# Attention in a fused network: value blocks moved by two steps, denominators before values, bf16 casts of q and k on ScalarE

## What is computed

```
x_ln = layer_norm(x_flat, g1, beta1)
qkv = x_ln @ w_qkv.T
q, k, v = jnp.split(qkv, 3, axis=-1)
...
scores = jnp.einsum('bhqd,bhkd->bhqk', q, k) * HEAD_DIM ** (-0.5)
attn = jax.nn.softmax(scores, axis=-1)
out = jnp.einsum('bhqk,bhkd->bhqd', attn, v)
```

## Time and profile before

| | us |
|---|---|
| median of three runs | 3499.21 (3495.88 to 3499.93) |
| the profiled execution | 3492.03 |
| its span, first to last instruction | 3490.3 |
| attention: ACT's first exponential to its last | about 102 to 1792 |
| one middle period of attention | 52.37 |

### The profile page before, as it was taken

How to read it: one execution, slowest core, us unless ns; L and a number is a source line. 1 busy time by engine, 2 the same in 40 slices (tenths; PEclk the granted TensorE clock), 3 DMA queues, 4 the chain that set the end, 5 groups by cost and what they waited for, 6 DMA issues and landing times. The chain is left out here.

```text
span 3490.3 us, 54609 instructions
## 1 busy us (share of the span) xinstructions
PE 3056.1 (88%) x17526; PEld 1156.3 (33%) x17526; DVE 2526.1 (72%) x3282; ACT 2045.6 (59%) x2445; POOL 2163.6 (62%) x876
## 2 busy tenths in 40 slices
PE   5999999999999999999957999556887788877877
PEld 2333333333333333333312333422232222222222
DVE  4888888888788888888812221236898889898888
ACT  3577777777677777777732332235556545655554
POOL 0588888888778888888870000016666766676665
PEclk7899999999999999999979999778999999999999
DMA  3577777777767777777763210134343434434343
GB/s 108 121 170 173 185 170 178 184 172 172 172 168 177 176 179 172 176 185 173 170 149 111 94 42 12 63 116 152 124 154 126 146 129 143 146 127 163 109 158 121
DMA packets 111603, 503.25 MB, mean 144 GB/s; under 512 B 17184, under 2 KB 18276, under 8 KB 78516
## 3 DMA queue, kind: packets, MB, share of 16 engines
q0 software_dynamic: 32704, 218.17, 29.9%
q1 hardware_dynamic: 78676, 282.17, 23.5%
HBM read 192.42 MB, written 39.39 MB: 66 GB/s over the span
## 5 line engine op out<-in xcount | busy, mean ns | idle before, releaser
L565 DVE TENSOR_REDUCE at_pmax<-at_ring 128x1 f32<-128x512 f32 x2048 | 1289.2, 685 | 280.2 <-PE at_ring L356 279.0
L527 ACT ACTIVATE at_probs<-at_sc 128x1024 f32<-128x1024 f32 x1024 | 992.5, 1021 | 371.1 <-PE at_sc L423 369.6
L615 POOL TENSOR_TENSOR at_prob_sums<-at_prob_sums,at_probs 128x2048 f32<-128x2048 f32 x192 | 907.1, 4725 | 72.2 <-ACT at_probs L527 71.9
L416 PE MATMUL at_sc<-at_QT,at_KT 32*128 32x512 f32 x4096 | 774.4, 632 | 8.3 <-issue 7.1
L1695 POOL TENSOR_TENSOR ss_drive<-ss_du,ss_bsb 128x1024 f32<-128x1024 f32 x261 | 610.7, 2353 | 263.4 <-DVE ss_state L1652 256.6
L1595 ACT ACTIVATE ss_decay<-ss_delta,ss_a 128x512 f32<-128x512 f32 x520 | 354.5, 687 | 446.9 <-DVE ss_state L1648 298.9
L435 PE MATMUL at_O<-at_probs,at_V 128*32 128x512 f32 x4096 | 536.2, 607 | 1.1 <-ACT at_probs L527 1.1
L1484 PE MATMUL ss_Y<-ss_seen,ss_ident 128*128 128x512 f32 x1032 | 520.1, 628 | 0.0
L356 PE MATMUL at_ring<-at_KH,at_QH 32*128 32x512 bf16 x2048 | 430.1, 387 | 6.9 <-DVE at_pmax L565 4.0
L1660 DVE TENSOR_TENSOR ss_seen<-ss_state,ss_C 128x1024 f32<-128x1024 f32 x259 | 316.3, 1221 | 78.7 <-PE ss_C L1472 70.8
L1652 DVE TENSOR_TENSOR_SCAN ss_state<-ss_decay,ss_state,ss_drive 128x512 f32<-128x512 f32 x259 | 332.3, 1283 | 33.6
(11 more groups left out here) (195 smaller groups left out, 2847.7 us busy)
## 6 DMA issues: line engine op xcount, KB each, us to landing
ss_bsb<-scratch_rows SPq DMA_DIRECT2D x265, 512.0 KB, 6.9
at_odd_sums<-at_probs POOLq DMA_DIRECT2D x128, 1024.0 KB, 7.6
at_odd_sums<-at_probs SPq DMA_DIRECT2D x64, 1024.0 KB, 4.8
at_prob_sums<-at_odd_sums POOLq DMA_DIRECT2D x64, 1024.0 KB, 8.1
scratch_attn<-at_att SPq DMA_DIRECT2D x64, 256.0 KB, 2.0
fc_att<-scratch_attn SPq DMA_DIRECT2D x32, 512.0 KB, 5.8
ss_xn<-scratch_xm SPq DMA_DIRECT2D x34, 256.0 KB, 5.6
at_xn<-scratch_xn SPq DMA_DIRECT2D x32, 256.0 KB, 6.5
```

What stands on the lines that cost most here:

```text
L416: nc.tensor.matmul(sc[:, h, :], KT[head(h), par, blk(kb)], QT[head(h), par, hs(half)], start=True, stop=False)
L527: nc.scalar.activation(probs[:, kb, two, :].rearrange("p h q -> p (h q)"), sc[:, two, :].rearrange("p h q -> p (h q)"), ACT.Exp, scale=SCA ...
L565: nc.vector.tensor_reduce(pmax[:, quad // 2, h, quad % 2:quad % 2 + 1], ring[:, unit[3], :], AX_X, ALU.max, negate=True).then_inc(max_done, 1)
L615: nc.gpsimd.tensor_tensor(prob_sums[:, half, :, :], before, probs[:, POOL_ADDS[n], :, :], ALU.add).then_inc(pool_sums, 1)
```

## The change

Three edits, all in `attention_phase`.

`PV_AT` puts value block 1 of each half in step 3 rather than 2, and block 2 in step 4 rather than 3. Step 2 has one block, step 4 two.

In PE's period the denominators come before the step's value block. In step 0 q's projection comes after the value block; the other projections stay ahead of theirs.

The bf16 casts leave DVE. ACT writes them from the ring just before its f32 copy, and no longer waits for `cast_done`, which it now raises itself.

```diff
-    PV_AT = {0: (LAST_KB,), 2: (0, 1), 3: (2,), 4: (3,), 5: (4,), 6: (5,), 7: (6,)}
+    PV_AT = {0: (LAST_KB,), 2: (0,), 3: (1,), 4: (2, 3), 5: (4,), 6: (5,), 7: (6,)}
...
                     for kind, which in extra.get(s, []):
-                        if kind in MADE_AHEAD:
+                        if kind in MADE_AHEAD and kb:
                             project(stage, grp, par, kind, which)
+                        if kind == "den" and stage != "lead":
+                            denominators(stage, grp, which)
                     if stage != "lead":
                         for k in PV_AT.get(kb, ()):
...
                         if kind == "turn":
                             turn(stage, grp, which)
-                        if kind == "den" and stage != "lead":
-                            denominators(stage, grp, which)
+                        if kind in MADE_AHEAD and not kb:
+                            project(stage, grp, par, kind, which)
...
                 act.wait_ge(extra_ready, unit_count(stage, grp, unit))
-                if unit[1] in MADE_AHEAD:
-                    act.wait_ge(cast_done, casts(grp, *unit[1:3]))
                 nc.scalar.activation(to, ring[:, unit[3], :], ACT.Copy).then_inc(extra_done, 1)
...
                         else:
+                            act.wait_ge(extra_ready, unit_count(stage, grp, unit))
+                            nc.scalar.activation({"q": QH, "k": KH}[kind][:, 1 - par, hs(which)], ring[:, unit[3], :],
+                                                 ACT.Copy).then_inc(cast_done, 1)
                             take(stage, grp, unit, {"q": QT, "k": KT}[kind][:, 1 - par, hs(which)])
...
-                    for kind, which in extra.get(s, []):
-                        if kind in MADE_AHEAD:
-                            cast(stage, grp, par, kind, which)
```

More of the change, by code:

```diff
@@ L573, in combine @@
                 nc.vector.tensor_reduce(negm[:, four, :, 0], pmax[:, four, :, :], AX_X, ALU.min).then_inc(negm_done, 1)
[L575 to L581, removed]
             def period(grp, par, stage):
```

## The result

| | before | after |
|---|---|---|
| median, 15 executions each | 3495.88 us | 3507.29 us (3502.39 to 3514.25) |
| the profiled execution | 3492.03 us | 3511.0 us |
| its span | 3490.3 us | 3509.3 us |
| one middle period of attention | 52.36 us | 52.70 us |

The ratio is 1.003 with a 95% interval of 1.0023 to 1.0038, so the change costs 8 to 13 us. The periods account for it: 31 x 0.34 = 10.5 us.

What follows compares the result with a forecast made beforehand. It took PE's own pace and the wait for ACT's exponentials as the bound, not DVE. q's 0.27 and k's 0.05 gave 31 x 0.32 = 10 us, so 3509 from the median 3499.2, own range 3506 to 3521.

Steps and rivals of the forecast that it cites:

- q, second half: Step 9: ACT does V's copy, q's cast and q's copy in line, freeing the ring slot later; cost 0.27 us a period.
- the loop through ACT: One score buffer: heads 2 and 3 wait for the previous step's exponentials, loading 3.38 us after that step's start.
- k, first half: Step 1: k's cast and copy follow V's copy on ACT, freeing the ring slot later; cost 0.05 us a period.
- The 0.04 that step 0 gives back: Step 0: ACT's copy of q starts at 789.82 instead of 789.86, subtracted from k's ring-slot time in step 1.
- the second k: Step 3: k's copy on ACT done near 799.8, ring slot needed at 800.5; cost 0.
- Step 0: q's projection behind the value block, with its cast on ACT: ACT's copy starts at 789.82 instead of 789.86; taken as 0.
- The value blocks: Blocks moved from steps 2 and 10 towards 4 and 12: still queued behind waiting scores, filling no wait; gain 0.
- The denominators: Steps 6 and 14, ahead of the values: the sum's DMA lands in time, hidden by 2.9 us in the median; taken as 0.
- A: Rival: the moved value block fills PE's waits; 3489 us in one half (chance 0.16), 3468 in both (0.08).
- B: Rival: ACT's casts are hidden in its idle time; 3499 to 3505 us, chance 0.18.
- C: Rival: DVE was the bound, so four casts fewer save 2.4 us a period; 3425 us, chance 0.02.
- D: Rival: denominators wait for the sum's DMA, with values queued behind; +15 us on the forecast, 3524, chance 0.06.

## Why the prediction was right

1. **The whole.** Forecast +0.32 a period, measured +0.34; forecast 3509, measured 3507.29. The last agreement is partly luck: the forecast stood on a median of three runs, 3499.2, and all 15 of the kernel before, with these three, have 3495.88. The difference is the fair measure, +10 forecast and +11.4 between the medians.
2. **q, second half: 0.27.** Measured 0.26 by the experiment with this cast on DVE. Each link is in the rows: copies in line, slot later by 0.26, step 11 one block behind, the loop through ACT at 3.37.
3. **k, first half: 0.05.** Measured 0.08. From V's copy to the load of the maxima's weights are 796.63 - 795.00 = 1.63 in the kernel after and 794.00 - 792.45 = 1.55 before, so 0.08 where the working had 0.10. The 0.04 that step 0 gives back, subtracted there, did not reach this place: V's copy stands behind the exponentials and starts 3.21 after step 1's start in both kernels (792.45 - 789.24 and 795.00 - 791.79). For the second k the 0 is right, but the 799.8 in its working is where its copy starts (799.90 before, 0.60 long), not where it is done.
4. **Step 0: 0.** Right for the two edits together. Apart, they cost 0.21 and, with k's cast in it, about 0.3.
5. **The value blocks: 0.** Right as an edit alone, and for the reason given: they stand behind the waiting scores. What the text did not see is their cover for the denominators.
6. **The denominators: 0.** Right in the sum, wrong in the step. I looked at the DMA that finishes the sum, and no wait for it was added in the middle periods. The second thing that L408 waits for, a ring slot, was never looked at. Alone it costs 0.34, and the change escapes it only because the values are spread too: 52.69 with the denominators alone, 53.04 in the change without the spread, 52.70 in the change with or without the denominators' move. Had the two edits come apart, a forecast by this step would have missed by 10 us.
7. **The profiled execution.** Forecast 3502, it was 3511.0. Attention is 17.6 longer in it: 30 periods x 0.34 = 10.2, the period behind the loop's jump 58.12 - 53.91 = 4.2, the last period 56.12 - 52.98 = 3.1. Outside attention lie 1.4 more, where nothing was changed. In the two odd periods PE's granted clock was lower (0.88 for 0.95, 0.85 for 0.94), and no term of the sum had that. How much of it is in the median can't be told: 31 x 0.34 = 10.5 alone lies inside the measured 8 to 13 us, and the execution of before that was profiled was the fastest of its 15. But the spread goes with the clock: of the 15 executions after, the three with a granted clock of 0.946 over the whole span took 3502.39 to 3503.12 us, the one with 0.941 3514.25, and the profiled one had 0.942.

Of the rivals, A fell with the value blocks alone (52.36) and B with the 0.26 shown above; C fell with k's cast alone, and with the waits on DVE at 334.3 us for 335.0 although its busy time in each period fell from 43.1 to 40.8. For C the advice of the Trainium skill ("Perfetto Trace Analysis", section "Optimization Strategies"), to speed up the engines that block the matmul engine when it is idle, was weighed. These runs show where it must not be read off the wait list: the 335.0 us were waits of weight loads, while the matmuls behind them stood idle 1.7 us. D's DMA wait didn't show in the middle periods of the changed kernel or with the denominators alone; in the latter a wait of the same instruction on another resource does.

## What to carry to other kernels

In a loop in which several engines pass one small buffer around, price an edit by where it stands in the queue of the engine that frees the buffer, and not by busy shares. Moving q's read ahead of V's was worth 0.39 us a period with no work removed, while casts taken off the "blocking" engine gained nothing, neither one (52.35) nor all four (52.92). In these runs a price ended at the next wait: follow it through one wait more than the one you change (0.38 came instead of 0.66, 0.56 instead of 0.80). And when an instruction is moved ahead, list everything it waits for, since one edit may be free only because another covers it.

## What the runs showed of the hardware

Two things I had not expected. Behind the sixteenth of the 32 periods, where the hardware loop begins its second pass, PE issues nothing for some 7 us, in both kernels: its weight loads stop at the last maxima of a period and go on 7.44 us later before, 7.12 after. Weight loads of the kernel before:

```profile
949.54 0.75 PEld L416 LDWEIGHTS at_sc<-at_QT,at_KT 32*128 32x128 f32 x8 [7.44 <-issue]
```

And of the kernel after:

```profile
952.79 0.74 PEld L416 LDWEIGHTS at_sc<-at_QT,at_KT 32*128 32x128 f32 x8 [7.12 <-issue]
```

Around that stand PE's granted clock falls to 0.50, which is 1.2 of 2.4 GHz, and stays there while PE works again. Stretch views of before and of after:

```profile
949.50:957.00 7.50, 7.46 (x30) 2.65 (x34) 2.07 (x4) 2.53 (x4) 2.14 (x2) 0.50 0.62 126
```

```profile
952.10:969.50 17.40, 16.70 (x74) 6.29 (x74) 6.28 (x10) 8.78 (x12) 2.79 (x2) 0.50 0.47 125
```

The low clock, with its part inside the stand, lasted 10.2 us before and 20.5 after. It was long in the kernels that have both ACT's casts, all or three of the four, and q's projection behind the values in step 0 (the period behind the jump took 57.1 to 58.5 us in all six), and short in those that have neither or only one (52.8 to 54.8 us in seven, the kernel before among them). Why it lasts longer there isn't settled: each kernel has one traced execution, and no run changed this stretch alone.

The second is small. Three copies of ACT in line start 0.47 to 0.50 apart, whether they last 0.60, 0.59 and 0.60 us (step 0 with the casts alone) or 0.60, 0.62 and 0.63 (steps 1 and 9 of the changed kernel), so the duration of one doesn't tell when the next can start. Why the latter last longer isn't settled.
